# Shared-expert units placed one by one between the last steps of the second attention, with logits and scaled copies moved

## The reference

```
x = x + tanh(g_xattn[1]) * attention1(layernorm(x), ctx)        # 16 heads, own keys (100) and context keys (361)
h = layernorm(x)
shared  = gelu(h @ sW1 + sb1) @ sW2 + sb2                        # 256 -> 1024 -> 256, all tokens
weights = softmax(h @ gW + gb); the 3 largest of 15 are kept
routed  = sum over the kept experts of weight * expert(h)        # 256 -> 512 -> 256 each
x = x + tanh(g_ffn[1]) * (shared + routed + h)
```

## Time and profile before

| what | value |
|---|---|
| median of 3 runs | 1288.38 us (1286.13 to 1289.64) |
| the profiled execution's own time | 1287.16 us |
| its span in the profile | 1285.5 us |
| PE busy | 1184.4 us (92%) |
| DVE, ACT, POOL busy | 601.0, 478.9, 395.2 us |
| mean clock granted to PE | 0.95 of full speed |

### The profile page before, as it was taken

How to read it: one execution, slowest core, us unless ns; L and a number is a source line. 1 busy time by engine, 2 the same in 40 slices (tenths; PEclk the granted TensorE clock), 3 DMA queues, 4 the chain that set the end, 5 groups by cost and what they waited for, 6 DMA issues and landing times.

```text
span 1285.5 us, 28924 instructions
## 1 busy us (share of the span) xinstructions
PE 1184.4 (92%) x11336; PEld 910.6 (71%) x11336; DVE 601.0 (47%) x1377; ACT 478.9 (37%) x1130; POOL 395.2 (31%) x408
## 2 busy tenths in 40 slices
PE   6999999956999999956799999999997989999998
PEld 4767777644999999933466666666665569999985
DVE  5777777654210101065556666566544921221216
ACT  3545555412323232213344445454443323233221
POOL 3666666622222221121100111011011145555520
PEclk9999999867999999966899999999897999999999
DMA  6011113005989989440200100000000329999965
GB/s 183 25 31 31 32 31 120 16 14 199 356 321 333 323 317 331 179 130 1 71 14 14 31 20 24 21 20 20 2 8 14 143 85 363 356 350 357 343 230 173
DMA packets 64370, 180.91 MB, mean 141 GB/s; under 512 B 10156, under 2 KB 36588, under 8 KB 55788
## 3 DMA queue, kind: packets, MB, share of 16 engines
q1 hardware_dynamic: 55068, 156.40, 35.4%
q0 software_dynamic: 8064, 22.03, 4.7%
q10 hardware_dynamic: 1104, 0.64, 0.2%
HBM read 163.11 MB, written 15.93 MB: 139 GB/s over the span
## 4 chain that ended last, share of the span: by engine, by line
PE 66%; POOL 11%; DVE 11%; issue 9%; ACT 1%; DMA 1%; POOLq 0%; SPq 0%; DVEq 0%; ACTq 0%
PE kept_psum L2052 16%; PE kept_psum L2061 16%; POOL at_sum L321 6%; PE kept_psum L1242 5%; PE kept_psum L1298 5%; PE kept_psum L1262 4%; PE kept_psum L1284 3%; PE kept_psum L1211 3%; PE kept_psum L1226 3%; POOL at_sum L324 2%; DVE at_negmax L981 2%; PE kept_psum L1708 2%; PE kept_psum L2078 2%; PE kept_psum L2041 2%; POOL at_vn L332 1%
## 5 line engine op out<-in xcount | busy, mean ns | idle before, releaser
L1996 ACT ACTIVATE ex_hT<-kept_psum,ex_w 128x128 f32<-128x128 f32 x464 | 132.3, 368 | 303.1 <-PE kept_psum L2052 167.6
L2052 PE MATMUL kept_psum<-ex_xT,ex_w 128*128 128x128 f32 x1856 | 223.7, 277 | 0.0
L2052 PEld LDWEIGHTS kept_psum<-ex_xT,ex_w 128*128 128x128 f32 x1856 | 216.8, 194 | 0.1
L2061 PE MATMUL kept_psum<-ex_w,ex_hT 128*128 128x256 f32 x928 | 213.9, 379 | 0.0
L1970 DVE TENSOR_TENSOR ex_yt<-kept_psum,ex_b 128x256 f32<-128x256 f32 x84 | 35.7, 425 | 353.9 <-PE kept_psum L2061 353.9
L2061 PEld LDWEIGHTS kept_psum<-ex_w,ex_hT 128*128 128x128 f32 x928 | 170.1, 190 | 19.7
L1835 POOL DMA_INDIRECT ex_results<-ex_yt,ex_to_row x84 | 82.8, 986 | 255.8 <-DVE ex_yt L1970 255.8
L1124 ACT ACTIVATE at_probs<-kept_psum 120x800 f32<-120x800 f32 (+2 forms) x128 | 101.2, 842 | 86.5 <-PE kept_psum L1268 86.4
L981 DVE TENSOR_REDUCE at_negmax<-kept_psum 100x2 f32<-100x722 f32 x128 | 115.4, 901 | 0.0
L532 ACT ACTIVATE at_probs<-kept_psum 120x800 f32<-120x800 f32 (+1 forms) x96 | 80.1, 836 | 74.2 <-PE kept_psum L651 74.1
L406 DVE TENSOR_REDUCE at_negmax<-kept_psum 120x8 bf16<-120x800 f32 (+1 forms) x96 | 90.6, 985 | 27.2 <-PE kept_psum L642 26.7
(11 more groups left out here) (247 smaller groups left out, 1707.9 us busy)
## 6 DMA issues: line engine op xcount, KB each, us to landing
ex_w<-in_pack_in SPq DMA_DIRECT2D x32, 1028.0 KB
ex_w<-in_pack_out SPq DMA_DIRECT2D x32, 1024.0 KB, 7.9
ex_w<-in_pack_in SPq DMA_DIRECT2D x52, 514.0 KB
ex_w<-in_pack_out SPq DMA_DIRECT2D x52, 512.0 KB
at_ctx<-in_ctxT SPq DMA_DIRECT2D x31, 361.0 KB, 3.6
ex_normed<-ex_xhat SPq DMA_DIRECT2D x16, 200.0 KB
ex_xhat<-ex_results SPq DMA_DIRECT2D x8, 400.0 KB
ex_ways<-ex_results SPq DMA_DIRECT2D x6, 400.0 KB
```

Source lines behind the costliest of these rows:

```text
L1996: last = act.activation(hT[t % N][:, c, :], ps_h[:, (t * U + u) % N, i * P:(i + 1) * P], ACT.Gelu, bias=w1[t % N][:, B1 + c:B1 + c + 1])
L2052: last = pe.matmul(ps_h[:, (t * U + u) % N, i * P:(i + 1) * P], w1[t % N][:, c * ff + f:c * ff + f + P], xT[t % N][:, c, :], start=(c == 0 ...
L2061: last = pe.matmul(ps_y[:, t % N, 0:D], hT[t % N][:, c, :], w2[t % N][:, c * D:(c + 1) * D], start=(c == 0), stop=(c == FC - 1))
```

## The change

`late_tensor` and `late_scalar` are no longer called in `attend1`; what they did is written out in the steps, and five units of group 0 are placed one by one: unit 0 at t = 16 between `turn_sums` and `turn_mix`, unit 1 at the same place of t = 17, units 2 and 3 around the logits of pair 6, and unit 4 at t = 19 between the turns and the logits of pair 7. The logits of pair 5 go ahead of `project_out` of batch 14. On ACT the scaled copy of pair 7 goes from t = 18 to behind the copies of pair 7's turns. The mixture's own list begins with unit 5 instead of 4.

```diff
@@ scalar(act), step t
             if on(t + 2):
                 take_own(t + 2)
+            if B <= t <= B + 1:
+                prep.early_scalar(act, range(t - B, t - B + 1))
...
             p = pair_at(t + 1)
-            if p is not None:
+            if p is not None and p < PAIRED - 1:
                 prep.scale_normed(act, p)
             if on(t):
                 exponents(t, 3)
-            if t >= B:
-                late_scalar(act, prep, psum, t)
+            if t == B:
+                prep.take_logits(act, PAIRED - 3, psum[:, 3, :])
             if t == B + 1:
-                prep.early_scalar(act)
+                prep.take_turn(act, PAIRED - 2, 0, psum[:, 2:4, :])
+                prep.take_turn(act, PAIRED - 2, 1, psum[:, 4:6, :])
+                prep.early_scalar(act, range(2, 3))
+                prep.take_logits(act, PAIRED - 2, psum[:, 3, :])
+                prep.early_scalar(act, range(3, 4))
+            if t == B + 3:
+                prep.take_turn(act, PAIRED - 1, 0, psum[:, 2:4, :])
+                prep.take_turn(act, PAIRED - 1, 1, psum[:, 4:6, :])
+                prep.scale_normed(act, PAIRED - 1)
+                prep.early_scalar(act, range(4, 5))
+                prep.take_logits(act, PAIRED - 1, psum[:, 3, :])
@@ tensor(pe), step t
                 turn_sums(t - 2, 1)
+            if t == B:
+                pe.wait_ge(exp_done, B * UNITS * HALVES)
+            if B <= t <= B + 1:
+                prep.early_tensor(pe, range(t - B, t - B + 1))
...
                 turn_mix(t - 2)
+            if t == B:
+                prep.logits(pe, PAIRED - 3, psum[:, 3, :])
...
                 values_own(t)
-            if t == B:
-                pe.wait_ge(exp_done, B * UNITS * HALVES)
-            if t >= B:
-                late_tensor(pe, prep, psum, t)
             if t == B + 1:
-                prep.early_tensor(pe)
+                pe.wait_ge(prep.logits_taken, PAIRED - 2)
+                prep.turn(pe, PAIRED - 2, 0, psum[:, 2:4, :])
+                prep.turn(pe, PAIRED - 2, 1, psum[:, 4:6, :])
+                prep.early_tensor(pe, range(2, 3))
+                prep.logits(pe, PAIRED - 2, psum[:, 3, :])
+                prep.early_tensor(pe, range(3, 4))
+            if t == B + 3:
+                pe.wait_ge(prep.logits_taken, PAIRED - 1)
+                prep.turn(pe, PAIRED - 1, 0, psum[:, 2:4, :])
+                prep.turn(pe, PAIRED - 1, 1, psum[:, 4:6, :])
+                prep.early_tensor(pe, range(4, 5))
+                prep.logits(pe, PAIRED - 1, psum[:, 3, :])
@@ the mixture's own lists
-                shared_gelu(act, 0, range(FS // 2, FS))
+                shared_gelu(act, 0, range(5, FS))
...
-                shared_hidden(pe, 0, range(FS // 2, FS))
+                shared_hidden(pe, 0, range(5, FS))
```

More of the change, by code:

```diff
@@ L2145, in main @@
         if shared:
-            prep.early_tensor = lambda pe: shared_hidden(pe, 0, range(FS // 2))
-            prep.early_scalar = lambda act: shared_gelu(act, 0, range(FS // 2))
+            prep.early_tensor = lambda pe, fs: shared_hidden(pe, 0, fs)
+            prep.early_scalar = lambda act, fs: shared_gelu(act, 0, fs)
         fed = Fed(ways_loaded, add_last, add_ways, weight_last, summed, finished, drained)
```

## The result

| | before | changed |
|---|---|---|
| median of 7 runs | 1286.21 us (1282.30 to 1289.64) | 1276.81 us (1273.51 to 1279.97) |
| span of the profiled execution | 1285.5 us | 1275.1 us |
| ratio to before, 95% interval | | 0.9937 [0.9915, 0.9959] |

The changed kernel is faster, by 0.6%. The ratio is worth 8.1 us of 1286.21 (5.3 to 10.9).

The account below looks back on a forecast made before the run. PE's work bounds the loop; gain lies before `rank()`, set by PE's units and DVE's mask. 8.15 less 0.4 gives 7.75 us: 1279.4 from the profiled execution, 1280.6 from the median; predicted 1280.0 us, range 1276.5 to 1285.0.

Parts of the forecast that it names:

- `rank()`'s shift is the end's shift: Behind `rank()` no engine's order changes and PE's 1.66 us wait in `table()` moves along, so its shift reaches the end.
- The rival of a loop paced by transfers: Loop over the tiles: DMA sets the pace and the gain is given back, 1286 to 1288 us; chance 0.06.
- Step 16 costs nothing: Unit 0 hides in the 1.42 us wait before `turn_mix`, pair 5's logits take the 0.52 wait; projection starts at 968.25.
- Step 17: Unit 1 fits before `turn_mix` at 971.9, projection ends at 974.0; residual of batch 15 gains 2.1 us.
- The clock holds in steps 16 and 17: Clock stays 1.00 through 969 to 981; rival that it falls anyway gives 1283.5 to 1284.5 us, chance 0.12.
- `take_logits` of pair 7 ends at 981.2: After pair 7's turns, unit 4 and logits; DVE's route starts at 981.25 instead of 989.36, 8.1 us earlier.
- Route to mask 12.44 us, 0.4 of it more contention: DVE's route took 12.04 us before; POOL's additions could hold its own by 0 to 0.8 more, 0.4 taken; mask at 993.7.
- Unit 7 waits 2.1 us: PE waits for Gelu 5, queued behind the Exp and its table load and ending at 986.05: new wait of about 2.1 us.
- The clock falls there with even odds, 0.4 us: A fall at unit 7's wait would make `rank()` 0.8 to 1.0 us later; half counted, 0.4.
- The mask binds, not PE: PE reaches `rank()` at 992.9, before the mask at 993.7, and waits 0.9 us.
- Table switch: On ACT, a switch with work ahead costs 1.3 us; the skill adds a 1.38 us drain, 2.66 in all.
- The rival with a drain: ACT's table switch also costs a drain, delaying Gelu 0 and unit 7: 1.2 us together, 1281.2 us; chance 0.03.

Follow-up runs that it names:

- the run with the addition held: Changed kernel with GpSimd's second addition of pair 6 held until the last mix is done: stretch 27.90 us, ratio 0.9942.
- The blank units: Kernel before, with matmuls whose result is unused added in the two waits of steps 16 and 17, block of four units kept: stretch 32.07 us, ratio 0.9973.
- empty waits: Changed kernel with no units in the two waits, units 0 and 1 around pair 6's logits, unit 2 before pair 7's: stretch 31.25 us, ratio 0.9959.
- The table of two by two: Stretches with block of four or split units, waits empty or blank-filled: block 37.03 and 32.07 us, split 31.25 and 30.09 us.
- unit 4 back: Changed kernel with unit 4 alone back in the mixture's list: stretch 28.68 us, ratio 0.9935.
- the joined units: Changed kernel with units 2 and 3 as a block behind pair 6's logits and unit 4 back in the mixture's list: 28.99 us, ratio 0.9963.
- scaled copy back: Changed kernel with pair 7's scaled copy back at step 18, ahead of the copies of pair 7's turns: stretch 28.24 us, ratio 0.9939.
- both repairs: Changed kernel with GpSimd's second addition of pair 6 held until the last mix and pair 7's scaled copy back: stretch 27.76 us, ratio 0.9929.
- the logits of pair 5 back: Changed kernel with pair 5's logits behind `project_out` of batch 14 again: stretch 28.37 us, ratio 0.9957.

## Why the prediction was right

It said 1280.0 us (1276.5 to 1285.0), and a shift of `rank()` by 7.75 us in the profile. Measured were 1276.81 us, and 8.66 us in the stretch. To compare times of the changed trace with the forecast's, 1.77 us are added, by which its first row here is earlier than in the earlier trace rows.

- *`rank()`'s shift is the end's shift*: right. From its start to the end of the span it is 283.5 us before and 283.54 after, and PE's 1.66 us wait in `table()` stayed. Not every execution passes it on so exactly: in five of the experiments the rest took 285.2 to 285.6 us (last section). The rival of a loop paced by transfers falls: 194.37 us busy of 195.10.
- *Step 16 costs nothing*: right. Unit and logits fill the waits; the projection starts at 967.95 by the old clock of the trace, forecast 968.25.
- *Step 17*: right in its end, residual at 974.18 against 974.0, by errors of opposite sign, which is luck in part. The transposes ended 0.2 us sooner than I put them (970.25 against 970.45), and the mix took 0.94 us instead of 0.43. That cost is shown by the run with the addition held: 0.47 us of the stretch.
- *The clock holds in steps 16 and 17*: right, 1.00. The blank units show that filled waits are enough for it. That units are needed in both is not shown, since with empty waits and the logits of pair 5 moved the clock held until 974.
- *`take_logits` of pair 7 ends at 981.2*: 981.26.
- *Route to mask 12.44 us, 0.4 of it more contention*: mis-sized. It took 11.78 us (991.36 - 979.58), 0.26 less than before. I had added 0.4 us to a route that already held 0.77 us of this (the first addition, 1.18 us and not 0.41). Here GpSimd's second addition started after the route's first instruction, and held only the third, by 0.51 us.
- *Unit 7 waits 2.1 us*: right in kind, 1.16 us in size. The Exp came 1.92 us after the logits' copy, where I had 2.55, mostly for the same missing contention. That is 0.63 of the 0.94 us.
- *The clock falls there with even odds, 0.4 us*: it did not fall. In none of the ten kernels that have this wait (1.01 to 1.65 us, with units on both sides) did it fall there. The prediction read from the earlier trace rows that such a fall had cost the kernel before about 2 us. The blank-unit kernel, with the same 1.49 and 0.44 us of waits around the last logits and no fall behind them, needs 12.71 us from their copy to `rank()` where the kernel before needs 12.72: without the fall PE waits 1.42 us ahead of unit 7 instead. So that fall was worth nothing there, and why it is absent here is open. This term of 0.4 and the route's 0.66 us are what the forecast of 7.75 lacks to 8.66, less small losses.
- *The mask binds, not PE*: right, 0.80 us of waiting, forecast 0.9.
- *Table switch*: a load of 1.28 us behind the Exp, which ended at 981.81, and the Gelu at 983.12. The rival with a drain falls here; the Trainium skill's figure in "ScalarE: Activation LUTs", What ACT_TABLE_LOAD costs, is not what this trace shows.

"GPSIMD Engine Reference", section 8, Key points, of the Trainium skill says that the shared interfaces contend when DVE has two SBUF inputs, and this trace agrees in detail. The addition of GpSimd ran from 979.71 to 981.11. The reduction within it, with one input, took 0.40 us as always, and the subtraction after it, with two, 0.92 instead of 0.41.

What the forecast did not see is how the parts overlap. It counted the clock and the split block as steps of one sum. The table of two by two shows that blank units alone give 5 of the 8.66 us and the split, with the moves that go with it, nearly 6. How much of this the move of the logits of pair 5 does for the clock is the rival left untested.

## What to carry to other kernels

Where PE idles in short waits, put ready work there one piece at a time, and no block ahead of something on which another engine's long chain waits. Look at the clock first: here useless matmuls in two waits of 1.4 us each made the stretch 5 us shorter. Two fixes of one stretch should be measured in all four combinations, since their gains may be the same microseconds, and each of the four should differ in nothing else. And when two engines meet at one point, as PE's units and DVE's mask do at `rank()`, moving work on one of them pays only down to the other's arrival: unit 4's place took 1.06 us of waits off PE (0.57 for ACT's copies, 0.49 behind the Exp), and 0.31 us off the stretch.

## What the runs showed of the hardware

- A GpSimd addition of 1.26 us held a DVE addition with both inputs in SBUF nearly until it was done: the last mix ran from 969.33 to 970.27 and not to 969.76, while GpSimd's ran from 968.72 to 969.98. In other rows DVE's likewise ended 0.27 us after GpSimd's (981.38 and 981.11 here, 990.54 and 990.27 in the kernel before). DVE's multiplication at 968.81, within the same GpSimd addition, has one input in PSUM and took 0.42 us as always. Placing the addition by one semaphore gave 0.47 us.
- Much of the noise comes from outside the changed code. The same code reached the start of the stretch at 957.13 us in one trace and at 966.79 us in another. Up to 950 us the mean clock was 0.95 in the five traces that reached it earliest, and 0.94 in the seven others. Behind `rank()`, seven traces took 283.4 to 284.1 us to the end. Five took 285.2 to 285.6 (blank units with the block, unit 4 back with and without the joined units, scaled copy back, both repairs), with the clock at 0.50 for some 3 us at the end of `table()`. With one trace of each kernel, whether the order of the work decides that stays open. Two views by stretches, of the kernel before and then of the earliest one:

```profile
240.00:330.00 90.00, 60.95 (x547) 48.85 (x536) 43.17 (x112) 22.21 (x54) 27.43 (x25) 0.73 0.31 114
```

```profile
240.00:330.00 90.00, 60.02 (x593) 48.65 (x586) 45.51 (x124) 22.71 (x56) 28.71 (x27) 0.81 0.37 135
900.00:955.00 55.00, 50.19 (x798) 35.36 (x801) 29.25 (x71) 24.87 (x45) 4.63 (x5) 1.00 0.02 6
```

  The first fence is the kernel before; the second, with the logits of pair 5 back, had the clock at 0.81 instead of 0.73 in that part, and at 1.00 late in the second attention. That the clock explains the whole of the 8 to 10 us is not shown. A term of half a microsecond is therefore to be read in the trace, not in the time.
